# Output steps of a decoder kernel: eight row buffers in place of four, rows of x loaded seven steps ahead instead of three

## What is computed

```
x = layernorm(x + hyena(x))        # this change is here
x = layernorm(x + ssm_attention(ctx, ctx, x))
x = layernorm(x + bitlinear_ffn(x))

hyena(u): xn = layernorm(u)*gamma + beta
          up = xn @ W_in.T + b_in           # 512 -> 1536 channels
          x0, x1, v = split(short_conv3(up))
          v  = v * x1
          y  = long_conv(v, k) + v*conv_bias
          return (y * x0) @ W_out.T
```

## Time and profile before

| | |
|---|---|
| median of 3 runs | 1024.22 us (1019.03 to 1025.34) |
| time of the profiled execution | 1022.91 us |
| span in its profile | 1020.8 us |
| mean granted TensorE clock | 0.984 |
| PE busy | 958.3 us, 94% |
| DVE busy | 814.6 us, 80% |
| ACT busy | 594.0 us, 58% |
| POOL busy | 503.2 us, 49% |
| output steps, rows 0 to 15 | 180.9 to 244.6 us (PE) |
| output steps, rows 16 to 31 | 388.9 to 446.5 us (PE) |
| second block starts | 460.25 us |

### The profile page before, as it was taken

One profiled execution on the slowest core, in us unless ns is written; L12 is line 12 of the kernel. 1 busy time (PEld: TensorE's weight loads), 2 busy tenths in 40 slices (PEclk: granted clock), 3 DMA queues, 4 the chain that ended last, 5 costly groups with the idle time before them and its releaser, 6 DMA issues.

```text
span 1020.8 us, 14172 instructions
## 1 busy us (share of the span) xinstructions
PE 958.3 (94%) x4299; PEld 559.5 (55%) x4299; DVE 814.6 (80%) x1636; ACT 594.0 (58%) x719; POOL 503.2 (49%) x790
## 2 busy tenths in 40 slices
PE   3899999999999999957999999999999999999995
PEld 2445545544355454325666666666666666666641
DVE  6977995678446666666899999999999999999872
ACT  4755544201565657501666777777767677677674
POOL 5410410122000001426877878787877778787851
PEclk9999999999999999987999999999999999999997
DMA  9323645364476678653447474655646474746333
GB/s 316 85 60 118 184 163 165 117 201 145 146 261 208 205 251 290 208 166 94 132 105 176 125 155 133 147 144 133 161 116 166 115 172 110 176 120 158 78 73 83
DMA packets 186921, 157.24 MB, mean 154 GB/s; under 512 B 100501, under 2 KB 141497, under 8 KB 184825
## 3 DMA queue, kind: packets, MB, share of 16 engines
q1 hardware_dynamic: 186872, 156.65, 55.3%
HBM read 101.88 MB, written 33.77 MB: 133 GB/s over the span
## 4 chain that ended last, share of the span: by engine, by line
PE 50%; DVE 2%; ACT 1%; POOL 1%; issue 1%; DMA 0%; POOLq 0%; DVEq 0%; ACTq 0%
PE conv_bank L1368 27%; PE hq_bank L1437 10%; PE back_bank L1456 5%; PE ff_bank L1456 5%; PE back_bank L1363 1%; PE back_bank L1428 1%; ACT hq_f L1525 0%; ACT g L1564 0%; DMA hq_t<-hq_int 0%; DVE z L1642 0%; POOL sum L1767 0%; ACT o L1550 0%; DVE block_diag L1146 0%; ACT qx L1140 0%; POOL sum L1771 0%
## 5 line engine op out<-in xcount | busy, mean ns | idle before, releaser
L817 DVE SCALAR_TENSOR_TENSOR conv_all<-u,taps,conv_all 128x1024 f32<-128x1024 f32 x92 | 122.4, 1331 | 93.5 <-ACT conv_all L689 91.6
L1767 POOL TENSOR_TENSOR sum<-z 128x512 f32<-128x512 f32 x128 | 163.0, 1273 | 7.5 <-DVE z L1642 7.5
L1368 PE MATMUL conv_bank<-block_diag 128*128 128x288 f32 x508 | 138.9, 413 | 2.8 <-DVE z L1642 2.8
L1368 PE MATMUL conv_bank<-kv,block_diag 128*128 128x288 f32 x512 | 138.4, 409 | 2.5 <-ACT conv_bank L1516 1.3
L1437 PE MATMUL hq_bank<-x_lo,hq_t 128*128 128x512 f16 x512 | 123.1, 385 | 4.0 <-DMA hq_t<-hq_int 4.0
L681 ACT ACTIVATE u<-slot_bank,bias,unscale 128x1024 f32<-128x1024 f32 x46 | 55.4, 1205 | 111.9 <-PE slot_bank L515 87.9
L552 PE MATMUL slot_bank<-wout_t,y 128*128 128x512 f32 x256 | 111.9, 594 | 1.6 <-DVE res L837 1.6
L1368 PEld LDWEIGHTS conv_bank<-block_diag 128*128 128x128 f32 x508 | 95.8, 194 | 29.8 <-DVE z L1642 4.8
L1368 PEld LDWEIGHTS conv_bank<-kv,block_diag 128*128 128x128 f32 x512 | 93.7, 190 | 31.1 <-DVE z L1642 5.4
L1771 POOL TENSOR_TENSOR sum<-sum 128x256 f32<-128x256 f32 x128 | 94.4, 738 | 10.1
L515 PE MATMUL slot_bank<-x_lo,w_hi 128*128 128x512 f16 x384 | 92.3, 383 | 3.2 <-DVE x_lo L805 3.2
(11 more groups left out here) (174 smaller groups left out, 1692.9 us busy)
## 6 DMA issues: line engine op xcount, KB each, us to landing
block_diag<-in_ctx_turned SPq DMA_DIRECT2D x32, 512.0 KB, 3.7
x_quad<-in_w_t SPq DMA_DIRECT2D x10, 1024.0 KB, 8.1
v_scratch<-conv_all SPq DMA_DIRECT2D x16, 512.0 KB, 3.2
c_scratch<-v_tok SPq DMA_DIRECT2D x8, 1024.0 KB, 5.2
y<-c_scratch SPq DMA_DIRECT2D x8, 1024.0 KB, 5.0
res<-in_x SPq DMA_DIRECT2D x32, 256.0 KB, 2.9
x_scratch<-res SPq DMA_DIRECT2D x32, 256.0 KB, 3.1
block_diag<-ssm_scratch SPq DMA_DIRECT2D x32, 256.0 KB, 4.9
```

What stands on the lines that cost most here:

```text
L817: ins = nc.vector.scalar_tensor_tensor(out=acc, in0=(u_first[kind] if n < 3 else u)[:, t0 + tap:t0 + tap + T // 2, :].rearrange("p t b -> ...
L1368: last = nc.tensor.matmul(view(conv_bank[tb % 2][:, hh, :], 0, (ROW64, T // 2), (1, PAIRS)), toep[:, head.buf, window * P:(window + 1) * P ...
L1767: nc.gpsimd.tensor_tensor(sum2[:, :, :].rearrange("p t (s j) -> p t s j", j=HD), view(z[:, b, :, :], 0, (SEGS * SEG, T), (SEG, half), (1, ...
```

## The change

The buffer `res` gets eight rows of 512 floats per partition in place of four (16 KB in place of 8), with as many semaphores `res_loaded` and `res_stored`; every `R % 4` and `R // 4` of a row buffer becomes `R % 8` and `R // 8`. SP loads row R + 7 at step R in place of row R + 3, and seven rows ahead of the first half's steps in place of three. The load at step R still reuses the buffer of row R - 1 and still waits for its store. The last step that has a load is 24 in place of 28. [...]

```diff
+RES = 8
-        res_loaded = [sem(f"res_loaded{i}") for i in range(4)]
+        res_loaded = [sem(f"res_loaded{i}") for i in range(RES)]
                 def load_res(R):
                     hf, t = divmod(R, T)
-                    if R >= 4:
-                        sp.wait_ge(res_stored[R % 4], 16 * (R // 4))
-                    sp.dma_start(res[:, R % 4, :], dram["x"][t, b_rows(hf), :]).then_inc(res_loaded[R % 4], 16)
+                    if R >= RES:
+                        sp.wait_ge(res_stored[R % RES], 16 * (R // RES))
+                    sp.dma_start(res[:, R % RES, :], dram["x"][t, b_rows(hf), :]).then_inc(res_loaded[R % RES], 16)
...
                 sp.wait_ge(w_turned, EC)
-                load_res(0)
-                load_res(1)
-                load_res(2)
+                for R in range(RES - 1):
+                    load_res(R)
                 bring_back(0, 2)
...
-                        for i in range(4):
-                            sp.wait_ge(res_stored[i], 16 * (T // 4))
+                        for i in range(RES):
+                            sp.wait_ge(res_stored[i], 16 * (T // RES))
...
                         R = hf * T + t
-                        if R + 3 < HALF * T:
-                            load_res(R + 3)
+                        if R + RES - 1 < HALF * T:
+                            load_res(R + RES - 1)
                         store_res(R)
...
-                    dve.wait_ge(res_loaded[i], 16 * (R // 4 + 1))
+                    dve.wait_ge(res_loaded[i], 16 * (R // RES + 1))
...
-        early["res"] = sb("res", [P, 4, D])
+        early["res"] = sb("res", [P, RES, D])
...
-    nc = _bacc.Bacc("TRN2", target_bir_lowering=False, num_devices=1)
+    nc = _bacc.Bacc("TRN2", target_bir_lowering=False, num_devices=1, dynamic_dma_scratch_size=1024)
```

More of the change, by code:

```diff
@@ L289, in store_res @@
                     sp.wait_ge(res_normed, R + 1)
-                    sp.dma_start(dram["x1_scratch"][t, b_rows(hf), :], res[:, R % 4, :]).then_inc(res_stored[R % 4], 16)
+                    sp.dma_start(dram["x1_scratch"][t, b_rows(hf), :], res[:, R % RES, :]).then_inc(res_stored[R % RES], 16)
                 def regroup(hf, cc):
@@ L833, in res_stat @@
                 def res_stat(R):
-                    i = R % 4
+                    i = R % RES
                     dve.wait_ge(out_full, R + 1)
-                    dve.wait_ge(res_loaded[i], 16 * (R // 4 + 1))
+                    dve.wait_ge(res_loaded[i], 16 * (R // RES + 1))
                     nc.vector.tensor_tensor(res[:, i, :], slot_bank[R // 2 % 2][:, R % 2, :], res[:, i, :], ALU.add).then_inc(res_added, 1)
@@ L1314, in store @@
                     sp.dma_start(dst, o[:, head.c % FAR, :]).then_inc(stored[head.c % FAR], 16)
-                for i in range(4):
-                    sp.wait_ge(early["res_stored"][i], 16 * (HALF * T // 4))
+                for i in range(RES):
+                    sp.wait_ge(early["res_stored"][i], 16 * (HALF * T // RES))
                 def turn_xq(head):
@@ L1859, in build @@
         early["conv_bank"] = [ctx.enter_context(nc.psum_tensor(f"conv_bank{i}", [P, 2, 512], F32)) for i in range(2)]
-        early["res"] = sb("res", [P, 4, D])
-        early["res_stored"] = [ctx.enter_context(nc.semaphore(f"res_stored{i}")) for i in range(4)]
+        early["res"] = sb("res", [P, RES, D])
+        early["res_stored"] = [ctx.enter_context(nc.semaphore(f"res_stored{i}")) for i in range(RES)]
         with ExitStack() as first:
```

## The result

The changed kernel took 1010.55 us (median of 4 runs, 1004.84 to 1011.01) where the kernel before took 1022.56 us on the same chip (4 runs, 1019.03 to 1025.34). The ratio is 0.9872, with a 95% interval of 0.9822 to 0.9921. 1010.0 us were forecast. The profiled execution took 1011.01 us, with a span of 1009.0 us; it is 11.9 us shorter than the profiled execution of before.

The account below looks back on a forecast made before the run. Late row loads on SP's load-store beat were taken to hold DVE and the first block's end. 12.1 + 0.5 + 1.0 + 0 = 13.6 us off 1022.9 gives 1009.3, off the median 1010.6; said 1010, range 1005 to 1018 (8 in 10).

Parts of the forecast that it names:

- The second half's steps and the tail: End of first block: second block starts 12.1 us sooner, 2.7 from PE's stalls and 9.4 from its idle time.
- The first half's steps: First block's first half: weights for slot 3 come sooner, worth 0.5 us, bounds 0 and 1.4.
- The clock: First head, after the block's change: less time at half clock, worth 1.0 us, bounds 0 and 2.9.
- a short fall: First head: the clock still falls to half rate after the shorter idle pieces, but briefly; convolution in 7 to 9 us.
- The four extra loads: Ahead of the first half's steps: four more row loads before `v_ct` cost nothing, upper bound 4.0 us.
- The beat lengthens: Rival, chance 0.12: SP's steps lengthen, rows 24 to 31 come late; 1015 at 4.5 us a step, 1022 at 5.5.
- The tail is hidden: Rival, chance 0.12: something besides DVE ends the first block, so only 2.7 + 0.5 us count; 1019 to 1021.
- Slower: Case, chance 0.04: the changed kernel as a whole is slower, by over 1%.

Follow-up runs that it names:

- e9: The change itself run again, on one chip beside two variants of it: 1010.88 us, ratio 0.9896 to the kernel before.
- e2: Against the kernel before: six row buffers and loads five ahead, with the change's `dynamic_dma_scratch_size=1024`; 1017.96 us, ratio 0.9962.
- e1: The kernel before with only `dynamic_dma_scratch_size=1024` added, still four buffers and loads three ahead: 1021.49 us, ratio 0.9989.
- e7: The change itself run again, on the same chip as its variants: 1007.19 us, ratio 0.9854 to the kernel before.
- e3: Against the kernel before: five row buffers, loads still three ahead, so a load waits for the store of step R - 2; 1007.61 us, ratio 0.9865.
- e6: The change with the early loads of rows 3 to 6 put off until just before the steps: 1004.84 us (one run).
- e10: The change with loads five ahead in place of seven, eight buffers, a load waiting for the store of step R - 3: 1005.03 us, ratio 0.9832.
- e8: The change with loads three ahead in place of seven, eight buffers, a load waiting for the store of step R - 5: 1009.40 us, ratio 0.9868.

## Why the prediction was right, point by point

**The second half's steps and the tail: right, to 0.1 us.** 12.1 us were forecast, and 12.09, 12.08 and 12.08 us stand in the three traces of the change (59.30, 59.31 and, in e9, 448.42 - 389.11 = 59.31 us from the start of B to the block's change, where before it was 71.39). Its parts came as said: 128 matmuls in one piece, and the 4.18 us from the last add to the change, which e2 and the change repeat as 4.17. The 1.3 us of idle time that is left lies in the 1 to 2 forecast. The mechanism is shown, not only the number: in e2 the add of row 31 is late again and the block's change with it.

**The first half's steps: the waits came as said, the term did not.** PE's wait for the third quad went, and PE reached the slots 1.85 us sooner, counted from the start of A (61.93 us in place of 63.78). Then it waited for the weights, as said: 2.9 us at slot 3 were forecast, and 4.03, 2.74 and 1.81 were seen, 2.86 on average. The step that failed is "SP's loads and stores there are on the same beat in both kernels". The weights were to go out at 254.34, that is 73.5 us into A; they went out at 76.0, 75.6 and 73.3. The reading behind it was that only the store of row 9 waited for DVE, and that its wait held SP up. But the store of row 10 waited too (the load at step 10 of the kernel before, the store, the next load):

```profile
236.13 0.33 SPq L285 DMA_DIRECT2D res<-in_x  x1
237.91 0.33 SPq L290 DMA_DIRECT2D x_scratch<-res  x1
239.92 0.33 SPq L285 DMA_DIRECT2D res<-in_x  x1
```

And neither wait held SP up by its length. These two stores, issued 1.7 and 1.8 us behind a load, let the next load go after 2.02 and 2.01 us; of the other stores from row 2 on, 0.37 us behind a load, most took 2.95 to 3.25. So steps 9 and 10 took 239.92 - 232.42 = 7.50 us, and in the change, where no store waited there, 7.30. What moves most from one trace to the next is one landing, that of row 6's store behind a 1 MB load of `x_quad`: 5.83 us before, 5.34 in e1, and 6.74, 6.70 and 4.79 in the three of the change. From the weights' time, and because 1.74 us of half clock follow slot 3 in the trace of before and in the first of the change but not in e7 and e9, stretch A came out 0.17 us longer, 2.92 shorter and 3.58 shorter than in the trace of before. The forecast 0.5 with bounds 0 and 1.4 holds none of the three. Nor does the kernel before have one value: e1 runs the same instructions in 203.13 us for 208.00. A term built on a beat of 3.5 us over 15 steps carries 0.1 us a step 15 times, and bounds of 1.4 us were too narrow for it.

**The clock: undersized, and by a wrong reason for its size.** 1.0 us was forecast for the first head, and no run shows that term. It was a little less than what its own rows gave: 5.9 us at half clock from 464.11 to 470 lose half of that, 2.95 us; 3.4 us at half clock, as behind slot 3, would lose 1.7, and the difference is 1.25. Two traces of the change have 1.75: 1.29 in the convolution, and 0.46 in the four transposes ahead of it (1.09 to 0.63 us), which the sum had left out. The third has 0.12 + 0.46 = 0.58; its convolution took 9.92 us, outside the 7 to 9 that were given as a sign. The forecast of a short fall was right for the first trace of the change:

```profile
454.00:456.00 2.00, 2.00 (x7) 1.42 (x8) 2.00 (x2) 0.00 (x0) 1.92 (x2) 0.71 0.50 131
456.00:458.00 2.00, 2.00 (x6) 1.41 (x5) 1.79 (x5) 0.59 (x1) 0.61 (x3) 0.50 0.72 178
```

PEclk is 0.71 and 0.50 in these windows, and 0.94 in the next. But the length of the fall does not follow that of the idle time. After 10.72 and 10.95 us of it the same 28 matmuls took 10.04 and 9.30 us (before, e1), after 7.86 us 8.66 (e2), after 2.17 us 9.44 (e3), and after 1.30 us 8.75, 8.75 and 9.92 (the change, e7, e9). Mean PEclk over these matmuls was 0.70 and 0.75, then 0.81, then 0.74, and 0.80, 0.80 and 0.71: some half clock stands behind the idle time in each, and the idle time sizes none of it.

**The four extra loads: some 0.3 us, not 0.** The term is small, but it doesn't look like nothing (e6). The times to landing of `v_ct` did not show it: 6.2, 6.4 and 6.5 us (least, median, most), as before. PE's wait did.

**The rivals.** *The beat lengthens*: its premise came half true. Seven steps took 3.77, 3.54 and 3.86 us each, and in two of the three traces row 31's load had 0.2 to 0.3 us left of the 2.8 that were counted (443.15 + 2.9 for an add at 446.27; in e9 441.05 + 2.9 for 444.25). What uses it up is a single late landing near the end: 4.60 us for the last step here and 5.01 in e9. No trace shows a fall over that edge, but its 0.12 was no overestimate. What made those last landings late is open. *The tail is hidden*: refuted by e2. *Slower*, at 0.04: refuted by the ratio of 0.9872, and `dynamic_dma_scratch_size=1024` alone gave 0.9989 (e1); SP's wait for line 1556 of ACT, over 32 heads, is 215.1 us with the change for 215.3.

**The sum.** 12.1 + 0.5 + 1.0 + 0 = 13.6 us was forecast against the profiled execution. The three timings gave 12.0, 14.7 and 11.0 us off the median of before, 12.6 on average. The profiled pair differs by 11.9, since its changed execution entered stretch A 2.1 us late. So the total is right through its large term. That the small terms partly cancel, 0.75 too little for the clock in two traces and 0.3 too little for the loads, is luck, and the first half's term is below what single traces can tell. Luck, too, is how near the time itself came: 14.2 us were to go from a median of 1024.2, and 12.0 went from one of 1022.56.

**What the prediction saw and did not use.** It said that the load waits for the store just issued and called that SP's beat; it took the beat as given. e3 shows that it was the cause as much as the lead was: let the load wait for an older store, and one more buffer does what four did, within the intervals.

## What to carry to other kernels

When loads and stores of a ring of buffers share one in-order queue, ask which store the load waits for. With lead + 1 buffers it is the store just issued; with lead + 2 it is an older one, and here that single buffer (e3) was worth as much as four more rows of lead. Give both (e10) if the memory is there. A wait that a change lengthens far downstream, like the one for weights queued behind the last store, is found by following what stands behind the steps on the same queue. And a wait of the queue is not a cost by its length: here two stores that had waited landed about 1 us sooner (the next load went 2.0 us behind them, and 2.95 to 3.25 behind most others). Before a term of 1 us is argued, look at how far that stretch moves between two executions of the same kernel.

## What the hardware showed that was not expected

- Whether half clock followed a gap of 2 to 3 us changed from one execution to the next. The gap at slot 3 was followed by half clock at 2.03 us (before, PEclk 0.51 from 268.9 to 272.3), at 3.07 (e2, 0.60 from 269 to 273) and at 4.03 us (the change, 0.68 from 269.8 to 275.2), and not at 2.74 (e7), 1.81 (e9), 1.04 (e6) and 0.42 us (e1), where PEclk was 1.00 from there to 280 us:

```profile
268.34 1.90 PE L515 MATMUL slot_bank<-x_hi,w_hi 128*128 128x512 f16 x8 [0.42 <-ACT conv_all L689]
```

- A store of one row (256 KB) issued well behind a load landed sooner. In the first half's steps of the nine traces with the coupling, a store 0.37 us behind a load let the next load go after 2.9 to 3.6 us (3.7 to 6.7 for rows 3 and 6, behind a 1 MB load), and one over 1.2 us behind it after 2.0 to 2.3. The medians from issue to landing agree: 3.1 us before and 3.3 with the change, 2.2 in e3 and e8, 2.4 in e10, while the loads' is 2.9, 3.0, then 2.9, 3.4 and 3.8. In e3 half of the stores come 1.6 us or more behind a load, when DVE has the row. No run varied this distance by itself.
- The first store of the second half's steps took 9.4 to 10.4 us to land in every trace with the coupling (9.7 before, 10.4 with the change); 1 MB of weights and the heads' loads were issued around it. e8's row 19 shows the same from the loads' side. That landing is the longest the ring has to cover.
